# Norming the transposed input on GpSimd in a two-block transformer kernel

## The reference, cut

```python
x  = x + attn_block(ln(x))                 # linear attention, then a GELU MLP 256-1024-256
x  = x + ffn_block(ln(x))                  # 256-1024 ternary weights, gelu, layer norm, 1024-256 ternary

def attn_block(x):
    xn = layer_norm(x, ln1_w, ln1_b)
    Q = elu(xn @ q_w.T + q_b) + 1          # 64 features
    K = elu(xn @ k_w.T + k_b) + 1
    V = xn @ v_w.T + v_b
    x = x + causal_linear_attn(Q, K, V) @ o_w.T + o_b
    h = gelu(layer_norm(x, ln2_w, ln2_b) @ f1_w.T + f1_b)
    return x + h @ f2_w.T + f2_b
```

## Time and profile before

| | us |
|---|---|
| median of 3 runs | 459.44 (459.27 to 460.21) |
| profiled execution | 459.38 |
| its span, first to last instruction | 457.6 |
| TensorE busy | 441.3, 96% |
| VectorE busy | 372.4, 81% |
| ScalarE busy | 323.0, 71% |
| GpSimd busy | 187.1, 41% |
| TensorE clock granted | 1.00 throughout |

### The profile page before, as it was taken

The page is one execution under the profiler, slowest core; times in us unless marked ns, Lnnn a source line. Parts: engine busy times, 40 slices in busy tenths (PEclk is TensorE's granted clock), DMA queues, the critical chain, the costliest instruction groups (busy, mean ns, idle before and its releaser), DMA issues.

```text
span 457.6 us, 8944 instructions
## 1 busy us (share of the span) xinstructions
PE 441.3 (96%) x2990; PEld 399.6 (87%) x2990; DVE 372.4 (81%) x1212; ACT 323.0 (71%) x604; POOL 187.1 (41%) x188
## 2 busy tenths in 40 slices
PE   3898999999999999999999999999999999999997
PEld 3786897999989899889989999889998899888977
DVE  6899888867898679986798778987799778876776
ACT  4896856997379854998469963898469885686163
POOL 3887042543247043540537041560536323370333
PEclk9999999999999999999999999999999999999999
DMA  8333000000010002000020002000020000000001
GB/s 237 120 106 127 0 2 1 1 25 1 24 46 25 2 0 70 2 23 1 2 69 2 24 1 69 2 25 1 0 71 2 23 1 9 17 1 23 1 24 47
DMA packets 10061, 14.09 MB, mean 31 GB/s; under 512 B 800, under 2 KB 9120, under 8 KB 9504
## 3 DMA queue, kind: packets, MB, share of 16 engines
q1 hardware_dynamic: 10016, 13.52, 8.9%
HBM read 9.32 MB, written 4.19 MB: 30 GB/s over the span
## 4 chain that ended last, share of the span: by engine, by line
PE 83%; issue 5%; DVE 4%; POOL 2%; DMA 2%; ACT 1%; SPq 1%; POOLq 0%; ACTq 0%
PE bank_f L425 13%; PE bank_p L473 11%; PE bank_y L208 6%; PE bank_y L209 6%; PE bank_y L439 6%; PE bank_y L210 6%; PE bank_f L208 5%; PE bank_f L209 5%; PE bank_f L210 5%; PE bank_a L208 4%; PE bank_a L210 4%; PE bank_a L209 4%; PE bank_a L216 2%; DMA x_odd<-in_x 2%; PE bank_f L216 2%
## 5 line engine op out<-in xcount | busy, mean ns | idle before, releaser
L1188 POOL TENSOR_TENSOR rs<-ve,neg_half 128x2 f32<-128x2 f32 x48 | 33.7, 702 | 204.0 <-DVE ve L872 196.6
L208 PE MATMUL bank_y<-wf_hi,h_hi 128*128 128x256 f32 x240 | 67.2, 280 | 0.0
L209 PE MATMUL bank_y<-wf_lo,h_hi 128*128 128x256 f32 x240 | 67.1, 280 | 0.0
L210 PE MATMUL bank_y<-wf_hi,h_lo 128*128 128x256 f32 x240 | 67.1, 279 | 0.0
L933 DVE TENSOR_TENSOR h_lo<-bank_f,h_hi 128x512 fp32r<-128x512 f32 x60 | 41.2, 686 | 27.5 <-ACT h_hi L686 27.4
L473 PE MATMUL bank_p<-wpj_t,g_hi 128*128 128x256 f32 x240 | 60.6, 288 | 0.0
L678 ACT ACTIVATE bank_f<-bank_f,f_bias 128x512 f32<-128x512 f32 x64 | 42.3, 661 | 25.4 <-PE bank_f L210 24.9
L1068 DVE SCALAR_TENSOR_TENSOR g_lo<-bank_y,vec,g_hi 128x256 fp32r<-128x256 f32 x128 | 55.0, 476 | 4.5 <-ACT g_hi L715 4.1
L473 PE MATMUL bank_p<-wpj_t,g_lo 128*128 128x256 f32 x240 | 58.6, 280 | 0.0
L715 ACT ACTIVATE g_hi<-bank_y,vec 128x256 fp32r<-128x256 f32 x128 | 53.5, 477 | 7.2 <-PE bank_y L439 3.8
L425 PE MATMUL bank_f<-wfc_t,z3T_hi 128*128 128x512 f32 x128 | 53.7, 420 | 0.8 <-DVE z3T_lo L933 0.8
(11 more groups left out here) (292 smaller groups left out, 1206.1 us busy)
## 6 DMA issues: line engine op xcount, KB each, us to landing
out<-y_yc SPq DMA_DIRECT2D x15, 256.0 KB, 2.2
x_even<-in_x SPq DMA_DIRECT2D x8, 256.0 KB, 2.9
x_odd<-in_x SPq DMA_DIRECT2D x8, 256.0 KB, 3.0
h<-in_f SPq DMA_DIRECT2D x1, 1024.0 KB, 8.0
y_yc<-in_f SPq DMA_DIRECT2D x1, 1024.0 KB, 10.4
h<-in_fc SPq DMA_DIRECT2D x1, 1024.0 KB, 4.7
h<-in_pj SPq DMA_DIRECT2D x1, 1024.0 KB, 4.9
z<-in_wv SPq DMA_DIRECT2D x1, 256.0 KB, 4.0
```

The lines of the kernel that those rows point to most:

```text
L208: pe.matmul(ps, w[0], r[0], start=start, stop=False, skip_group_check=skip)
L209: pe.matmul(ps, w[0], r[1], start=False, stop=False, skip_group_check=skip)
L210: return pe.matmul(ps, w[1], r[0], start=False, stop=stop, skip_group_check=skip)
L1188: pool.tensor_tensor(rs[n][:, 2 * h:2 * h + 2], ve[n][:, 2 * h:2 * h + 2], neg_half[:, 0:2], ALU.pow).then_inc(s[f"ln{n + 1}_rs"], 1)
```

## The change

The host lays x out a second time, for each group as 128 partitions x 2 x 512 tokens (feature k * 128 + p on partition p). Groups 0 and 1 are as before. From group 2 on:

- `u_norm`, `tu` and the old `u_lo` are gone. SyncE loads the transposed group into the memory of `u` (`xt`), 512 KB.
- The scale (`rs`) and shift (`sh`) of each token, one column per tile, are written by two DMAs of 4-byte pieces to a small tensor in device memory, and read back spread over all partitions into `lines_b` (`spread_lines`).
- GpSimd does x * scale (`x_mul`), minus shift (`x_add`; `ln1_shift` now gives mean * rs - 1, so the 1 is in it) and later the low part (`x_lo`), each a half at a time, 128x512. ScalarE's `u_hi` reads `xt` instead of a bank.
- `qk_mm` waits for `xt_lo`; `scores` waits for `z2_lo` of the group before, which held back `tu` until now.
- All lists are written anew: `first()` reaches two groups further for u, `step(g)` runs for g of 1 to 3, `last()` begins a group earlier. In a stage `qk_mm` of the next group stands one `f1` later.

```diff
+            def load_transposed(g):
+                if g == 2:
+                    sp.wait_ge(s["tu_done"], 4)
+                else:
+                    sp.wait_ge(s["xt_lo"], 2 * (g - 2))
+                sp.dma_start(xt, xt_d[g]).then_inc(s["xt_loaded"], 16)
+            def spread_lines(g):
+                sp.wait_ge(s["ln1_sh"], 4 * g + 4)
+                for n, a in enumerate((rs, sh)):
+                    sp.dma_start(lines_d[g % 2, n].rearrange("t p -> p t"), a[0][:, 1, :],
+                                 allow_slow_non_contiguous=True).then_inc(s["lines_out"], 16)
+                sp.wait_ge(s["lines_out"], 32 * (g - 1))
+                if g > 2:
+                    sp.wait_ge(s["xt_sum"], 2 * (g - 2))
+                sp.dma_start(lines_b[:].rearrange("p r n -> p (r n)"),
+                             lines_d[g % 2].rearrange("(a r) t p -> a (r t p)", a=1).to_broadcast([P, 2 * N])).then_inc(s["lines_in"], 16)
...
             def qk_mm(g):
-                pe.wait_ge(s["u_lo"], 2 * g + 2)
+                if g >= 2:
+                    pe.wait_ge(s["xt_lo"], 2 * (g - 2) + 2)
+                else:
+                    pe.wait_ge(s["u_lo"], 2 * g + 2)
...
             def u_hi(g, h):
+                if g >= 2:
+                    act.wait_ge(s["xt_sum"], 2 * (g - 2) + h + 1)
+                    act.wait_ge(s["v_done"], 2 * (g - 1) + h + 1)
+                    cols = slice(2 * h * P, (2 * h + 2) * P)
+                    act.activation(uT[0][:, :, cols], xt[:, :, cols], ACT.Copy).then_inc(s["u_hi"], 1)
+                    return
...
+            def x_mul(g, h):
+                cols = slice(2 * h * P, (2 * h + 2) * P)
+                pool.wait_ge(s["xt_loaded"], 16 * (g - 1))
+                pool.wait_ge(s["lines_in"], 16 * (g - 1))
+                pool.tensor_tensor(xt[:, :, cols], xt[:, :, cols], lines_b[:, 0:1, cols].to_broadcast([P, KD, 2 * P]),
+                                   ALU.mult).then_inc(s["xt_scaled"], 1)
+            def x_add(g, h):
+                cols = slice(2 * h * P, (2 * h + 2) * P)
+                pool.wait_ge(s["xt_scaled"], 2 * (g - 2) + h + 1)
+                pool.tensor_tensor(xt[:, :, cols], xt[:, :, cols], lines_b[:, 1:2, cols].to_broadcast([P, KD, 2 * P]),
+                                   ALU.subtract).then_inc(s["xt_sum"], 1)
+            def x_lo(g, h):
+                cols = slice(2 * h * P, (2 * h + 2) * P)
+                pool.wait_ge(s["u_hi"], 2 * g + h + 1)
+                pool.tensor_tensor(uT[1][:, :, cols], xt[:, :, cols], uT[0][:, :, cols].bitcast(F32),
+                                   ALU.subtract).then_inc(s["xt_lo"], 1)
```

The new stage on TensorE and GpSimd:

```diff
             def step(g):
-                f1(g, 0); proj(g - 1, 0, 2); tu(g + 1, 0); f1(g, 1); tr(g - 1, 1, 1); proj(g - 1, 0, 3)
-                tu(g + 1, 1); f1(g, 2); tr(g - 1, 1, 2); tr(g - 1, 1, 3); proj(g - 1, 1, 0); f1(g, 3); qk_mm(g + 1)
...
+                proj(g, 0, 2); f1(g + 1, 0); f1(g + 1, 1); tr(g, 1, 1); proj(g, 0, 3); f1(g + 1, 2); tr(g, 1, 2)
+                tr(g, 1, 3); f1(g + 1, 3); proj(g, 1, 0); f1(g + 1, 4); qk_mm(g + 2); f2(g + 1, 0); f2(g + 1, 1)
...
+                xs(g + 1); x_add(g + 2, 0); x_mul(g + 2, 1); ln4_rstd(g, 0); correct(g, 0); n1_rstd(g + 2)
+                x_add(g + 2, 1); x_lo(g + 2, 0); x_lo(g + 2, 1); ln1_rstd(g + 3, 0); ln4_rstd(g, 1)
+                ln1_rstd(g + 3, 1); n1o(g + 2); correct(g, 1); ln3_rstd(g + 1, 0); ln3_rstd(g + 1, 1)
+                x_mul(g + 3, 0); y_cpj(g + 1); ln2_rstd(g + 2, 0); xpb(g + 2); ln2_rstd(g + 2, 1)
```

More of the change, by code:

```diff
@@ L501, in last @@
-            def last():
[L503 to L518, removed]
@@ L520, in _ @@
             first()
-            for g in range(1, 6):
+            for g in range(1, 4):
                 step(g)
@@ L725, in first @@
[L725 to L729, removed]
@@ new lines, in first @@
+                g_lo(0, 0, 1); ln2_shift(1, 1); ln4_stats(0, 1); g_lo(0, 0, 2); ln4_var(0, 0); z2_lo(1, 0)
+                qk_max(2); z2_lo(1, 1); ln4_shift(0, 0); ln4_stats(0, 2); g_lo(0, 0, 3); qk_sum(2); g_lo(0, 1, 0)
+                output(0, 0); h_lo(1, 0); h_lo(1, 1); g_lo(0, 1, 1); qk_lo(2); h_lo(1, 2); g_lo(0, 1, 2)
+                g_lo(0, 1, 3); ae_mask(2); h_lo(1, 3); ad_mask(2); ln4_stats(0, 3); n1_shift(2); ln4_var(0, 1)
+                ae_lo(2); ad_lo(2); h_lo(1, 4); af_mask(2); ln1_stats(3, 0); ln4_shift(0, 1); h_lo(1, 5)
@@ new lines, in first @@
+                ln1_shift(3, 0); h_lo(1, 6); h_lo(1, 7); ln1_stats(3, 1); af_lo(2); v_lo(2, 0); ln1_shift(3, 1)
+                y_sum(1, 0); y_sum(1, 1); ln3_stats(1, 0); ln3_stats(1, 1); ln3_shift(1, 0); v_lo(2, 1)
+                ln3_shift(1, 1); attn_out(2, 0); attn_out(2, 1); ln2_stats(2, 0); ln2_stats(2, 1); z3_lo(1, 0)
+                z3_lo(1, 1); output(0, 1); ln2_var(2, 0); attn_out(2, 2); attn_out(2, 3); ln2_shift(2, 0)
+                ln2_stats(2, 2); ln2_stats(2, 3); ln2_var(2, 1); ln4_stats(1, 0); g_lo(1, 0, 0); ln2_shift(2, 1)
@@ L1265, in first @@
             def first():
[L1267 to L1271 removed]
+                consts(); ln1_rstd(0, 0); ln1_rstd(0, 1); n1_rstd(0); wf1_lo(0); ln1_rstd(1, 0); wf1_lo(1)
@@ new lines, in first @@
+                wf1_lo(2); n1o(0); wf1_lo(3); ln1_rstd(1, 1); wf2_lo(0); ln2_rstd(0, 0); ln2_rstd(0, 1); wf2_lo(1)
+                wf2_lo(2); wf2_lo(3); xpb(0); n1_rstd(1); xs(0); ln1_rstd(2, 0); ln1_rstd(2, 1); n1o(1)
+                ln3_rstd(0, 0); x_mul(2, 0); ln3_rstd(0, 1); x_add(2, 0); x_mul(2, 1); x_add(2, 1); x_lo(2, 0)
+                ln2_rstd(1, 0); x_lo(2, 1); y_cpj(0); ln2_rstd(1, 1); ln4_rstd(0, 0); n1_rstd(2); correct(0, 0)
+                xpb(1); xs(1); ln4_rstd(0, 1); correct(0, 1); ln1_rstd(3, 0); ln1_rstd(3, 1); n1o(2); ln3_rstd(1, 0)
@@ L1273, in step @@
+                ln3_rstd(1, 1); ln2_rstd(2, 0); x_mul(3, 0); y_cpj(1); ln2_rstd(2, 1); xpb(2)
             def step(g):
-                ln4_rstd(g - 1, 1); correct(g - 1, 1); n1o(g + 1); ln3_rstd(g, 0); ln3_rstd(g, 1)
-                ln2_rstd(g + 1, 0); y_cpj(g); ln2_rstd(g + 1, 1); ln1_rstd(g + 2, 0); ln1_rstd(g + 2, 1); xpb(g + 1)
-                n1_rstd(g + 2); ln4_rstd(g, 0); correct(g, 0); xs(g + 1)
+                xs(g + 1); x_add(g + 2, 0); x_mul(g + 2, 1); ln4_rstd(g, 0); correct(g, 0); n1_rstd(g + 2)
@@ L1283, in last @@
-                ln3_rstd(7, 0); correct(6, 1); ln3_rstd(7, 1); ln4_rstd(7, 0); y_cpj(7); correct(7, 0)
-                ln4_rstd(7, 1); correct(7, 1)
+                x_add(6, 0); x_mul(6, 1); xs(5); ln4_rstd(4, 0); x_add(6, 1); correct(4, 0); x_lo(6, 0); x_lo(6, 1)
+                n1_rstd(6); ln1_rstd(7, 0); ln1_rstd(7, 1); n1o(6); ln4_rstd(4, 1); correct(4, 1); x_mul(7, 0)
+                ln3_rstd(5, 0); ln3_rstd(5, 1); x_add(7, 0); x_mul(7, 1); y_cpj(5); ln2_rstd(6, 0); x_add(7, 1)
+                xpb(6); ln2_rstd(6, 1); n1_rstd(7); x_lo(7, 0); ln4_rstd(5, 0); correct(5, 0); x_lo(7, 1); xs(6)
@@ L1286, in _ @@
+                ln4_rstd(5, 1); correct(5, 1); n1o(7); ln3_rstd(6, 0); ln3_rstd(6, 1); ln2_rstd(7, 0)
+                ln2_rstd(7, 1); ln4_rstd(6, 0); y_cpj(6); correct(6, 0); xpb(7); ln4_rstd(6, 1); xs(7)
+                ln3_rstd(7, 0); correct(6, 1); ln3_rstd(7, 1); y_cpj(7); ln4_rstd(7, 0); ln4_rstd(7, 1)
+                correct(7, 0); correct(7, 1)
             first()
-            for g in range(1, 6):
+            for g in range(1, 4):
                 step(g)
```

298 lines of the change are left out of this document (193 added, 105 removed).

## The result

| | before | after |
|---|---|---|
| median of 5 runs | 459.27 us (458.92 to 460.21) | 494.47 us (493.29 to 495.48) |
| ratio | | 1.0751 [1.0732, 1.0771] |
| span of the profiled execution | 457.6 us | 493.1 us |
| TensorE matmuls, busy | 2990, 441.3 us | 2942, 449.6 us |
| mean granted TensorE clock | 1.00 | 0.97 |

A forecast was written before the change was run, and what follows sets the result against it. TensorE was taken to bound the kernel, busy 441.3 of 457.6 us. Removed transposes save 5.2 us, added GpSimd work, the trip and the start list cost 0: 459.4 - 5.2 = 454.2 us, range 452.2 to 458.2.

The forecast's parts named there:

- The gain, 5.2 us: On TensorE, 12 blocks of four u transposes removed at 0.44 us each, all on the path: 5.2 us saved.
- the busy sum: Sign that the forecast is right: TensorE's summed busy time falls by 5 us.
- Step (a): Scale and shift lines: two scattered writes, wait and spread read through device memory take 6 to 10 us, taken as 7.
- if the scattered writes take much more than a store: Stated condition under which the prediction falls; a store lands in 2.2 us.
- Rival B: Long device-memory trip holds x_mul at GpSimd's queue head; example 13.3 us trip, 12.5 us lost, 466.7 us; chance 0.06.
- The limit: At x_mul in GpSimd's queue, a trip up to 10.8 us is free; beyond, each us is lost once a group.
- The store behind SyncE's wait: store(g - 1, 1) in SyncE's queue, data ready at +7.2 us, not delayed unless the trip takes over 8 us.
- (c): GpSimd's queue through a stage: its last x_lo ends +33.2 to +33.4 us after y_sum(g, 0) starts.
- (d): qk_mm on TensorE comes at +33.6 us, x_lo ready 0.2 to 0.4 us before: no wait, thin margin.
- rival A: qk_mm waits for x_lo in each group from 3 on, 0.7 us in five groups: 457.7 us; chance 0.15.
- Rival C: Shared SBUF port: each GpSimd operation holds a VectorE operation up by 0.9 us; 12 us in six groups, 466 us; chance 0.03.
- The start list: Relisted kernel start gives the same TensorE waits within 1 us; taken as 0, bounds 2 us gain or loss.

The follow-up runs named there:

- experiment 1: Changed kernel without the trip: both writes and the spread read left out, lines_b filled with 1.0; 458.32 us, ratio 0.9958.
- 11: Changed kernel with 16-byte write pieces, GpSimd reading lines through a strided view, and the start list of the kernel before; 457.19 us, ratio 0.9950.
- 12: Changed kernel without the trip (no writes, no spread read, lines hold 1.0) and with the start list of the kernel before; 455.25 us, ratio 0.9913.
- far pieces: Changed kernel with its 1024 4-byte pieces a group landing 512 bytes apart, spread read taken from the transposed input; 457.6 us.
- one column: Changed kernel writing only the first of four columns, 128 adjacent 4-byte pieces a DMA, spread read from the transposed input; 473.4 us.
- experiment 3: Changed kernel with x_mul(., 0) moved behind ln2_rstd(., 1) in GpSimd's list, groups 3 to 6 only; 479.21 us, ratio 1.042.
- experiment 10: Changed kernel with 16-byte write pieces and GpSimd reading the lines through a view with a 16-byte step; 457.93 us, ratio 0.9971.

## Why the prediction was wrong, by its steps

- **The gain, 5.2 us: right.** 12 blocks at 0.44 us (5.3, to be exact). The stage is 0.9 us shorter with TensorE full, in experiment 1, and its matmul work over the whole kernel is 5.5 us less, start to start, in 11 and 12 (the busy sum, which I had named as the sign, falls by 4.3 us). Even so only 3.8 us were seen at best, since the start and the end keep gaps that the shorter lists don't remove.
- **Step (a), the trip taken as 7 us from a range of 6 to 10: wrong, and this is the step that failed.** It was 16.2 us. The read was 4.2 us, inside the bounds. The write was bounded at "2 us or less on top of 2.2" from 65 ns a packet, and took 11.3 us. That row is a mean over all packets of the kernel before, which writes nothing in small pieces to device memory, so it could bound the count of pieces but not what their neighbourhood costs. Nor is a packet's own time the term that grew: in the kernel after the recorded packets are over in a microsecond, and the wait comes behind them. Read as a count the estimate was fair: 1024 far pieces go in 2.0 us. The prediction itself named such a failure ("if the scattered writes take much more than a store"), yet gave it 0.06.
- **Rival B: the right mechanism.** Its marks are all there: idle time of GpSimd before `x_mul` ended by a DMA into lines_b, with `y_cpj`, `ln2_rstd`, `ln2_shift` and `z2_norm` late in that order. Its price for the measured trip would have been 5 x (16.2 - 10.8) = 27 us, 481 us. Three parts were off. (i) Six groups, not five, and two of them with another order of the queue, where the wait costs more: in `first()` and `last()` `x_mul` stands ahead of a power operation of the third norm. I had walked one stage only. (ii) The limit: with trips of 11.5 to 13.4 us (one column) the four middle groups lost 1.7 us in all, where a limit of 10.8 us gives 5.5, so it was too strict there. (iii) The clock, which the prediction held at full speed throughout.
- **The store behind SyncE's wait**, "not delayed unless the trip takes over 8 us": right as a condition, and experiment 3 met it.
- **Steps (c) and (d): right.** In experiment 1 `qk_mm` starts 33.6 us behind `y_sum` (171.84 to 205.46), as walked, and the last `x_lo` ends 0.5 us ahead of it. With GpSimd's chain some 0.8 us longer still (three strided operations in it at +0.28 us, experiment 10) TensorE still doesn't wait for `x_lo`, since idle moments in the queue take it up. So rival A had more margin against it than the 0.2 to 0.4 us of my walk.
- **Rival C: not seen.** In the kernel after, the one-column operations beside the GpSimd ones are where they were in the earlier trace rows, at 207 ns, and the stages of experiment 1 hold no idle time at all:

```profile
L968 DVE TENSOR_SCALAR sh<-mv,rs 128x1 f32<-128x1 f32 x96 | 15.8, 207 | 40.3 <-POOL rs L1320 40.0
```

- **The start list, taken as 0 with 2 us either way: off, at its bad end or past it.** Experiment 12 against 1 is 458.32 to 455.25, 3.1 us, or 2.1 us by the ratios. Walking the waits alone missed that a gap can also lower the clock: the runs of experiment 1 at a granted clock of 1.00 took 456.7 and 457.0 us, those at 0.993 458.3 to 458.8.

## What to carry to other kernels

Before a value is sent through device memory, look at how its pieces land, not only at how many they are: let one partition's values lie together (16-byte pieces here), or keep small pieces 16 or better 64 bytes apart, and put the reordering into the reader's view. An operation that waits for a DMA belongs behind the small operations of its queue that others wait for, and the place must be looked up in every list, first and last stages included. A trip with no row of its own in the trace wants a range as wide as its effect; here the write's 11 us alone decided the sign of the change.
